# An attention block on one core: VectorE takes the row maxima of two banks in one instruction, and the eight banks are dealt out anew

## The reference

```
qkv = jnp.einsum('bnc,dc->bnd', x, qkv_w) + qkv_b
q, k, v = (qkv[0], qkv[1], qkv[2])
attn = jnp.einsum('bhqd,bhkd->bhqk', q, k) * scale
attn = jax.nn.softmax(attn, axis=-1)
out = jnp.einsum('bhqk,bhkd->bhqd', attn, v)
```

## Time and profile before

| what | value |
|---|---|
| median of three runs | 5319.96 us |
| span of the profiled execution | 5315.8 us |
| attention stage, first full tile to last group's start | 1384 to 5045 us |
| TensorE busy, whole span | 5112.7 us (96%) |
| VectorE busy | 3462.7 us (65%) |
| ACT busy | 2575.9 us (48%) |
| GpSimd busy | 3517.1 us (66%) |

### The profile page before, as it was taken

The page is one execution under the profiler, slowest core; times in us unless marked ns, Lnnn a source line. Parts: engine busy times, 40 slices in busy tenths (PEclk is TensorE's granted clock), DMA queues, the critical chain, the costliest instruction groups (busy, mean ns, idle before and its releaser), DMA issues. The chain is left out here.

```text
span 5315.8 us, 82210 instructions
## 1 busy us (share of the span) xinstructions
PE 5112.7 (96%) x25420; PEld 2889.1 (54%) x25420; DVE 3462.7 (65%) x5616; ACT 2575.9 (48%) x4717; POOL 3517.1 (66%) x925
## 2 busy tenths in 40 slices
PE   8999999998999999999999999999999999999979
PEld 6878878787444444444444444444444444444447
DVE  4232232331887787788778877877887778778724
ACT  2121121211465666566666666665666666656641
POOL 1212212122588888888888888888888888888840
PEclk9999999999799999999999999999999999999989
DMA  5343343442302112120211202021120202020047
GB/s 172 93 146 107 102 143 102 128 127 79 83 17 53 40 28 49 25 49 17 51 34 38 49 23 51 17 49 27 47 49 19 55 17 49 21 53 17 7 151 240
DMA packets 186058, 348.31 MB, mean 66 GB/s; under 512 B 17956, under 2 KB 51748, under 8 KB 177448
## 3 DMA queue, kind: packets, MB, share of 16 engines
q1 hardware_dynamic: 185640, 342.99, 23.1%
HBM read 208.19 MB, written 134.22 MB: 64 GB/s over the span
## 5 line engine op out<-in xcount | busy, mean ns | idle before, releaser
L825 DVE TENSOR_REDUCE unit_max<-mx_ps 128x1 f32<-128x512 f32 x4096 | 2572.6, 679 | 771.7 <-PE mx_ps L887 746.5
L808 ACT ACTIVATE p_sb<-st_ps 128x512 f32<-128x512 f32 x4096 | 2206.5, 601 | 1292.3 <-PE st_ps L947 1276.5
L763 POOL TENSOR_TENSOR p_pair<-p_sb 128x2048 f32<-128x2048 f32 x512 | 2358.2, 4617 | 523.7 <-ACT p_sb L808 456.0
L887 PE MATMUL mx_ps<-k_x,q_x 96*128 96x512 f32 x4096 | 1798.6, 442 | 121.3 <-DVE unit_max L825 99.8
L947 PE MATMUL st_ps<-q_x,k_x 97*128 97x512 f32 x4096 | 1661.3, 409 | 3.0 <-ACT p_sb L808 3.0
L887 PEld LDWEIGHTS mx_ps<-k_x,q_x 96*128 96x128 f32 x4096 | 794.7, 194 | 1261.7 <-DVE unit_max L825 986.9
L899 PE MATMUL o_ps<-p_sb,v_sb 128*32 128x512 f32 x8192 | 1132.8, 626 | 0.7 <-ACT p_sb L808 0.7
L947 PEld LDWEIGHTS st_ps<-q_x,k_x 97*128 97x128 f32 x4096 | 788.5, 194 | 309.7 <-ACT p_sb L808 134.1
L753 POOL TENSOR_TENSOR p_pair<-p_pair 128x2048 f32<-128x2048 f32 x192 | 879.9, 4583 | 15.1
L285 POOL TENSOR_TENSOR h_lo<-h_f,h_hi 128x512 fp32r<-128x512 f32 x128 | 165.1, 1290 | 688.1 <-DVE h_hi L469 688.1
L469 DVE CAST h_hi<-h_f 128x512 fp32r<-128x512 f32 x128 | 55.0, 431 | 540.7 <-ACT h_f L342 540.7
(11 more groups left out here) (92 smaller groups left out, 3783.9 us busy)
## 6 DMA issues: line engine op xcount, KB each, us to landing
q_x<-q_hi_d SPq DMA_DIRECT2D x128, 256.0 KB, 5.4
k_x<-k_hi_d SPq DMA_DIRECT2D x30, 1024.0 KB, 9.6
xt<-x SPq DMA_DIRECT2D x64, 256.0 KB, 2.7
stage<-w SPq DMA_DIRECT2D x32, 512.0 KB, 4.9
q_hi_d<-qk_hi SPq DMA_DIRECT2D x64, 256.0 KB, 3.0
q_lo_d<-qk_lo SPq DMA_DIRECT2D x64, 256.0 KB, 3.8
k_hi_d<-qk_hi SPq DMA_DIRECT2D x64, 256.0 KB, 2.6
k_lo_d<-qk_lo SPq DMA_DIRECT2D x64, 256.0 KB, 3.3
```

What stands on the lines that cost most here:

```text
L763: pool.tensor_tensor(p_pair[:, slot, :, :], p_sb[:, 2 * i % SLOTS, :, :], p_sb[:, (2 * i + 1) % SLOTS, :, :], ALU.add).then_inc(pair_done, 1)
L808: act.activation(p_sb[:, kt % SLOTS, h, :], st_ps[(4 * kt + h) % 3][:, :], ACT.Exp, scale=SCALE).then_inc(exp_done, 1)
L825: dve.reduce_max(unit_max[:, n // 4, n % 4:n % 4 + 1], mx_ps[n % 3][:, :], AX.X).then_inc(unit_done, 1)
L887: pe.matmul(mx_ps[n % 3][:, :], q_x[qc][0:R, h, t * P:(t + 1) * P], k_x[u][0:R, h, kc * 512:(kc + 1) * 512], start=True, stop=True).then_i ...
```

## The change

VectorE reduces two units in one instruction: the banks of the maxima become two pairs (`mx_ps` is two tensors of two banks each), and a reduction writes two columns. It is issued at odd units and waits for the second of the two. On TensorE an even unit from 4 on waits until the pair that held its banks before is reduced; an odd unit waits for nothing. The fourth bank of the maxima comes from the scores, which have two banks, so a score waits for the exponential two before it. The transposed maxima still lie in `mx_ps[1]`, which now holds units 2 and 3, so the wait for their being read stands at unit 2.

```diff
-        st_ps = [ctx.enter_context(nc.psum_tensor(f"st_ps{i}", [P, TOK], F32)) for i in range(3)]
-        mx_ps = [ctx.enter_context(nc.psum_tensor(f"mx_ps{i}", [P, 512], F32)) for i in range(3)]
+        st_ps = [ctx.enter_context(nc.psum_tensor(f"st_ps{i}", [P, TOK], F32)) for i in range(2)]
+        mx_ps = [ctx.enter_context(nc.psum_tensor(f"mx_ps{i}", [P, 2, 512], F32)) for i in range(2)]
...
-                                act.activation(p_sb[:, kt % SLOTS, h, :], st_ps[(4 * kt + h) % 3][:, :], ACT.Exp,
+                                act.activation(p_sb[:, kt % SLOTS, h, :], st_ps[(4 * kt + h) % 2][:, :], ACT.Exp,
...
                 def unit(base, n):
 
-                    dve.wait_ge(unit_ready, base + n + 1)
-                    dve.reduce_max(unit_max[:, n // 4, n % 4:n % 4 + 1], mx_ps[n % 3][:, :], AX.X).then_inc(unit_done, 1)
-
-                def rows(base, count):
-
-                    dve.wait_ge(unit_done, base + UN)
+                    if n % 2:
+                        dve.wait_ge(unit_ready, base + n + 1)
+                        dve.reduce_max(unit_max[:, n // 4, n % 4 - 1:n % 4 + 1], mx_ps[n // 2 % 2][:, :, :], AX.X).then_inc(unit_done, 1)
+
+                def rows(done, count):
+
+                    dve.wait_ge(unit_done, done)
...
-                def unit(base, n, u, qc):
+                def unit(turn_done, n, u, qc):
 
                     h, t, kc = n // (4 * TT), n // 4 % TT, n % 4
-                    if n >= 3:
-                        pe.wait_ge(unit_done, base + n - 2)
-                    pe.matmul(mx_ps[n % 3][:, :], q_x[qc][0:R, h, t * P:(t + 1) * P], k_x[u][0:R, h, kc * 512:(kc + 1) * 512],
+                    if n >= 4 and n % 2 == 0:
+                        pe.wait_ge(unit_done, turn_done + n // 2 - 1)
+                    pe.matmul(mx_ps[n // 2 % 2][:, n % 2, :], q_x[qc][0:R, h, t * P:(t + 1) * P], k_x[u][0:R, h, kc * 512:(kc + 1) * 512],
                               start=True, stop=True).then_inc(unit_ready, 1)
...
-                            elif n == 1:
+                            elif n == 2:
                                 pe.wait_ge(shift_done, L * G + g + 2)
...
-                            pe.wait_ge(exp_done, since(L * G * SK, g * SK + (4 * kt + h - 2 if 4 * kt + h > 2 else 0)))
-                            pe.matmul(st_ps[(4 * kt + h) % 3][:, :], k_x[u][:, h, kt * P:(kt + 1) * P], q_x[qc][:, h, :],
+                            pe.wait_ge(exp_done, since(L * G * SK, g * SK + 4 * kt + h - 1))
+                            pe.matmul(st_ps[(4 * kt + h) % 2][:, :], k_x[u][:, h, kt * P:(kt + 1) * P], q_x[qc][:, h, :],
                                       start=True, stop=True).then_inc(st_ready, 1)
```

More of the change, by code:

```diff
@@ L776, in turn_shift @@
                         act.wait_ge(shift_ld, (count - 1) * 16)
-                    act.activation(shift[:, :], mx_ps[1][0:4 * TT, 0:P], ACT.Copy, scale=-1.0).then_inc(shift_done, 1)
+                    act.activation(shift[:, :], mx_ps[1][0:4 * TT, 0, 0:P], ACT.Copy, scale=-1.0).then_inc(shift_done, 1)
                 def copy_o(count):
@@ L848, in _ @@
                     unit(0, n)
-                rows(0, 1)
+                rows(UN // 2, 1)
                 for n in range(FIRST):
@@ L865, in turn @@
                                 if kt == AHEAD - 1:
-                                    rows(base, L * G + g + 2)
+                                    rows((L * G + g + ahead + 1) * (UN // 2), L * G + g + 2)
                             if 4 <= kt < 4 + INV and not (first and g == 0):
@@ L891, in turn_rows @@
                     pe.wait_ge(max_done, count)
-                    pe.transpose(mx_ps[1][0:4 * TT, 0:P], row_max[:, :], ident[:, :]).then_inc(rows_ready, 1)
+                    pe.transpose(mx_ps[1][0:4 * TT, 0, 0:P], row_max[:, :], ident[:, :]).then_inc(rows_ready, 1)
                 def values(L, n, u, kt):
@@ L920, in _ @@
                 for n in range(FIRST):
-                    unit(UN, n, 0, 1)
+                    unit(UN // 2, n, 0, 1)
                 def turn(L, first, last):
@@ L937, in next_unit @@
                                     pe.wait_ge(k_ld[nu], (L + (g + ahead) // G + nu) * 48)
-                            elif n == 1:
+                            elif n == 2:
                                 pe.wait_ge(shift_done, L * G + g + 2)
-                            unit((L * G + g + ahead) * UN, n, nu, nq)
+                            unit((L * G + g + ahead) * (UN // 2), n, nu, nq)
                         def scores(kt, h):
```

## The result

The changed kernel takes 5505.55 us in the median of four runs (5504.42 to 5509.03) against 5321.11 of the kernel before on the same chip: a ratio of 1.0347, with a 95% interval from 1.0333 to 1.0362. 5470 was forecast, with a range from 5400 to 5620.

A forecast was written before the change was run, and what follows sets the result against it. TensorE was taken to bound the attention stage, so VectorE gains count only where it waits. 61 × (4.5 − 1.1 − 1.1) = 140, + 9 + 2 = +151 us on 5315.8 gives 5467, with 4 around the span 5470; range 5400 to 5620.

The forecast's parts named there:

- The reduction of two banks: VectorE's merged reduction of 1024 elements takes 1.23 us; some 2 us of VectorE saved per group, counted as nothing for TensorE.
- The 0.3 us of tiles 5 to 7: In key tiles 5 to 7 units wait for a just-ended pair reduction: 0.1 us more in each of three tiles.
- Two banks for the scores: TensorE's scores wait for the exponential two before; with the pairs' 0.3 us, +4.5 us per group, bounds 2.5 and 6.
- Its second part, 0.05 us for the fourth score: Fourth score between two value products waits for the second one's exponential, streaming at 1.70 instead of 1.65 us.
- Tiles 13 and 15, put at nothing: No score-wait cost: tile 13 has two value products; in tile 15 TensorE waits for a unit anyway.
- The wait behind the normalisation: TensorE's unit wait after the normalisation shrinks from 1.8 to 0.7 us as GpSimd's addition ends earlier: −1.1 us per group.
- The clock: TensorE's clock stays at 2.4 GHz after the shorter wait in three groups of four: −1.1 us per group, bounds 0 and −1.5.
- The rival of the clock that still falls: TensorE's clock still falls after each 0.7 us wait, so 67 us more: 5540 us; chance 0.26.
- the one of the skill's rule: Short score waits themselves bring one more low-clock stretch per group, 1.5 us each: 5630 us or more; chance 0.09.
- The rest: Shift and units-only start: nothing; first two groups +4.6 us each, 9 together; last group +2.
- The 4 us around the span: Median of runs lies 4 us above the profiled span; taken as the same in both kernels, lifting 5467 to 5470.
- The rival "faster": Shorter wait and kept clock, worth 2.6 us a group, outweigh cheap score waits: 5257 us; chance 0.03.

The follow-up runs named there:

- run 6: The kernel before with the normalisation moved to GpSimd and two score banks instead of three, reductions single: 5489.4 us, ratio 1.0321.
- run 7: The changed kernel with the normalisation moved from VectorE to GpSimd: 5499.3 us, ratio 1.0339 to the kernel before.
- run 5: The kernel before with the normalisation moved from VectorE to GpSimd, three score banks kept: 5112.2 us, ratio 0.9609.
- run 4: The kernel before with ACT's wait for the score put last of the three before head 0's exponential: 5319.4 us, ratio 0.9999.
- run 3: The changed kernel with ACT's wait for the score put last of the three before head 0's exponential: 5463.0 us, ratio 1.0268.
- run 9: The changed kernel with TensorE's loop over two turns per pass, jumping back twice instead of five times: 5492.1 us, ratio 1.0326.

## Why the prediction was right

The sign, the place and the mechanism held. By its steps:

- **The reduction of two banks**: 1.23 us forecast, 1.225 in the median by the line's own row, and nothing gained on TensorE's path. The 0.3 us of tiles 5 to 7 measure 0.4 (runs 6 and 7), but only outside the loop; in the 48 looped groups they measure less than 0.1.
- **Two banks for the scores**: 4.2 us a group without the pair's share, 4.3 measured. The round trip of 1.18 us was the right row. Its second part, 0.05 us for the fourth score, hardly shows: a usual tile takes 0.26 us more in run 6 than in run 5, where 0.3 was forecast. Tiles 13 and 15, put at nothing, cost 0.14 and 0.26. That the sum comes out so near is in part luck.
- **The wait behind the normalisation**: 0.7 us forecast for every group; outside the loop 0.65 seen, and 0.5 by run 7. In the 48 looped groups only 0.18 us of idle time is left in most, and run 7 wins less than 0.1. The tie to GpSimd's addition held at 0.55 us for a third time, and the addition moved to 0.30 + 4.58 = 4.9 us behind the transpose, as forecast (4.8).
- **The clock**: I gave it back in three groups of four. It came back in all: the stage is at 1.00, and what low clock is left in it stands behind the five jumps. With that the step would have been −1.5 instead of −1.1. The rival of the clock that still falls is out, and so is the one of the skill's rule: the Trainium skill, page "TensorE: Matmul & The Clock Gate", section "A second HAM failure mode: psum-queue depth-cycling", has short idle times between matmuls swing the clock; here 26 score loads wait in most groups, and the granted clock of the stage is 1.00.
- **What was missing** is why the time is 35 us above the forecast. "The rest" priced nothing for ACT's waits in the loop. They were harmless before (run 4) and cost 43 us with two score banks (run 3), about 1 us in each of 48 groups. That 1 us is what is left of 1.8 (60.9 − 59.1 in run 6): the pairs and the wait behind the normalisation, forecast for all groups, hardly count beside it. And the five jumps cost some 5 us each, 25 in all, of which the kernel before showed about 1 each. The clock's better outcome took some 25 us off again (61 × 0.4): 43 + 20 − 25 = 38. That two costs which the forecast didn't have were half met by a better clock is luck: without the clock's part the forecast would have been some 60 us too low instead of 35.
- **The 4 us around the span** are 1.8: the profiled execution of the change took 5504.42 us at a span of 5502.6. The rest of the 4 was the spread between executions.

The rival "faster" was worth stating for its account: the wait and the clock were worth 3.5 us a group, even more than the 2.6 that it could have won.

## What to carry to other kernels

A buffer that looks idle may be what hides a round trip: before a bank is taken away, read the distance from a producer's start to the load that waits for its consumer (here 1.09 us), and lay it beside the time in which the other buffers are filled. Where VectorE and GpSimd both read two operands from SBUF, ask when the one lets the other go: here moving a single product of 0.25 MB per group from VectorE to GpSimd won 3.9%; merging 4096 instructions into 2048 won nothing on the path. And inside a loop, where an engine's wait values depend on the turn, the wait that comes last should stand last in its list. Where the values are fixed this doesn't hold: there the same order cost 0.4 us a group.

## What the runs showed of the hardware

- **The order of an engine's waits costs time**: with three waits before one exponential, two of them on values that depend on the loop's turn, the exponential started 0.57 to 0.59 us behind its score in most tiles, and 0.43 to 0.46 with the score's wait last (run 3). At one place a turn in tile 14 it was 0.97, elsewhere in that tile 0.68. Turning the order took 43 us off.
- **A jump back of TensorE's loop left it standing for 2.7 to 3.1 us** in the changed kernel (14.6 us for five), and for 1.9 to 4.1 in the other runs except the kernel before and run 4. Low clock follows it: 0.53 over 7 us behind one. A group with the jump took 4.2 to 5.4 us more than the same group without it (run 9).
- **VectorE's product of two SBUF tiles ends 0.55 us after a running GpSimd addition ends**, whatever it had waited: 2.94, 1.93 and 1.76 us in three places, and so for 63 of the 64 products in each of the two kernels (0.547 to 0.558 us). Alone it takes 0.69 (the minimum of its row). The Trainium skill, page "GPSIMD Engine Reference", section "1. Specifications", names contention of GpSimd with VectorE instructions that have two SBUF inputs. The trace agrees; that section doesn't say for how long, and here the product waits for the end of the whole addition. Reductions out of PSUM show no such wait: in run 5 four in a row take 2.48 us beside a running addition, 0.62 each.
